# Routing ten tiles one iteration sooner, keeping three tiles dense, and running sorted tiles between the pieces of the last cross attention

## What is computed

```python
x = x + self_attention(layernorm(x))          # 16 heads, causal, rotation over the whole head vector
x = x + cross_attention(layernorm(x), ctx)    # 16 heads of 32, over 722 rows
h = layernorm(x)                              # then a mixture of 8 experts, 2 of them for each token
gates = softmax(h @ gate_w.T + gate_b)
top_gates, top_idx = top_k(gates, 2)
out = einsum('bsh,eoh->bseo', h, expert_w) + expert_b
x = x + (take(out, top_idx) * top_gates).sum()
```

## Time and profile before

| what | us |
|---|---|
| median of 3 runs | 1271.86 (1271.14 to 1278.15) |
| profiled execution | 1280.48 |
| its span, first to last instruction | 1278.7 |
| PE busy | 1194.4 (93%) |
| VectorE, GpSimd, ScalarE busy | 830.7, 729.6, 642.2 |
| DMA | 93.28 MB, mean 73 GB/s |

### The profile page before, as it was taken

One profiled execution on the slowest core, in us unless ns is written; L12 is line 12 of the kernel. 1 busy time (PEld: TensorE's weight loads), 2 busy tenths in 40 slices (PEclk: granted clock), 3 DMA queues, 4 the chain that ended last, 5 costly groups with the idle time before them and its releaser, 6 DMA issues.

```text
span 1278.7 us, 43327 instructions
## 1 busy us (share of the span) xinstructions
PE 1194.4 (93%) x19120; PEld 806.8 (63%) x19120; DVE 830.7 (65%) x1455; ACT 642.2 (50%) x946; POOL 729.6 (57%) x690
## 2 busy tenths in 40 slices
PE   4789899999999999999999999999999877699997
PEld 4456576767667676767676767676767555555543
DVE  4658476858585867676767777677777586423156
ACT  4335556556565656565656464646565535533300
POOL 1436656667676766667675857575757455500042
PEclk9799999999999999999999999999999988799999
DMA  8010611010202010101011110101010345455356
GB/s 302 2 42 2 240 44 50 3 59 3 66 4 65 17 44 9 53 17 52 19 50 32 38 48 12 43 17 52 17 58 11 116 159 190 146 159 170 131 163 212
DMA packets 47840, 93.28 MB, mean 73 GB/s; under 512 B 3775, under 2 KB 15351, under 8 KB 47655
## 3 DMA queue, kind: packets, MB, share of 16 engines
q1 hardware_dynamic: 44135, 79.03, 18.7%
q0 software_dynamic: 3520, 11.47, 2.9%
HBM read 60.13 MB, written 30.36 MB: 71 GB/s over the span
## 4 chain that ended last, share of the span: by engine, by line
PE 86%; DVE 4%; DMA 3%; POOL 3%; ACT 2%; issue 1%; another core or an unknown queue 1%; SPq 1%; ACTq 0%; DVEq 0%
PE psum L323 56%; PE psum L922 7%; PE psum L1025 6%; PE psum L1010 5%; PE psum L940 2%; PE psum L899 2%; PE psum L891 1%; DMA bank<-in_L_attn_Wv 1%; DMA out<-bank 1%; PE psum L967 1%; PE psum L855 1%; PE psum L907 1%; DVE xT L1176 1%; POOL bank L1444 1%
## 5 line engine op out<-in xcount | busy, mean ns | idle before, releaser
L1444 POOL TENSOR_TENSOR bank<-prob,bank 128x1200 f16<-128x1200 f32 x128 | 314.6, 2468 | 188.4 <-ACT bank L1120 188.3
L1268 DVE TENSOR_REDUCE c_most<-psum 100x4 f32<-100x1444 f32 x128 | 211.6, 1653 | 14.7 <-PE psum L1010 12.6
L323 PE MATMUL psum<-bank,cT 128*128 128x512 f16 (+1 forms) x864 | 198.7, 379 | 0.1
L323 PE MATMUL psum<-cT,bank 128*128 128x361 f16 x1152 | 196.1, 321 | 0.0
L1111 ACT ACTIVATE prob<-psum 128x1200 f32<-128x1200 f32 x128 | 150.0, 1172 | 76.6 <-PE psum L1025 62.4
L1176 DVE TENSOR_TENSOR cv<-psum,cv 128x512 f16<-128x512 f32 x125 | 86.0, 688 | 107.4 <-ACT cv L1102 57.2
L1120 ACT ACTIVATE bank<-prob 128x1200 f16<-128x1200 f32 x128 | 151.7, 1198 | 1.4
L323 PEld LDWEIGHTS psum<-cT,bank 128*128 128x128 f16 x1152 | 106.1, 99 | 65.5 <-DVE c_raw L1195 3.0
L323 PEld LDWEIGHTS psum<-bank,cT 128*128 128x128 f16 (+1 forms) x864 | 85.1, 101 | 88.2 <-issue 4.1
L1102 ACT ACTIVATE cv<-psum 128x512 f16<-128x512 f32 x96 | 57.4, 598 | 149.9 <-PE psum L323 148.3
L1229 DVE SCALAR_TENSOR_TENSOR bank<-psum,b_part,bank 128x361 f16<-128x361 f32 x128 | 74.4, 592 | 81.1 <-ACT bank L1088 81.1
(11 more groups left out here) (215 smaller groups left out, 1905.8 us busy)
## 6 DMA issues: line engine op xcount, KB each, us to landing
c_raw<-in_ctx SPq DMA_DIRECT2D x16, 960.0 KB
xs_scratch<-y_kept SPq DMA_DIRECT2D x1, 7424.0 KB, 22.8
c_raw<-xs_scratch SPq DMA_DIRECT2D x29, 256.0 KB, 2.7
ys_scratch<-bank SPq DMA_DIRECT2D x29, 256.0 KB, 2.0
...
y_kept<-x_scratch SPq DMA_DIRECT2D x10, 256.0 KB, 3.2
```

Source lines behind the costliest of these rows:

```text
L323: last = pe.matmul(out_ap, a(pa), b(pb), start=(i == 0 and j == 0), stop=(i == len(pairs) - 1 and j == 2))
L1268: dve.tensor_reduce(c_most[:, hf], score[0:L, :, 0:HC], AXIS.X, ALU.max).then_inc(max_done, 1)
L1444: pool.tensor_tensor(prob16[o % 2][:, (2 + part) * PT:(3 + part) * PT], prob[:, part], prob16[o % 2][:, part * PT:(part + 1) * PT], ALU.su ...
```

## The change

Tiles 0 to 9 are routed, tile 10 (tokens 1280 to 1399, 120 rows) becomes dense with 11 and 12. So there are 27 slot tiles and 24 dense pieces. Tile 9 gets FS, FN, FX and FL in iteration 13. RT, RP and FR stand in steps 0 to 6 of iteration 14, SC0 to SC6 in its steps 8 to 19, and SC7 to SC9 in steps 0 to 3 of iteration 15. FW ends in step 14 there. Then ST0 to ST5 and SM0 to SM3 stand in steps 15 to 19, between the last group's pieces. SM is now a chunk in the four shared banks, copied out half by ACT and half by DVE. FS10 is in step 2 of iteration 15, FS11 in step 16. On SP, tile 10's load comes behind the four expert loads of iteration 15, then a wait for all scatters, x's store, tile 11's load and the slot loads; the reloads 4 to 9 move to iteration 14. Tiles 10 to 12 have buffers of their own for their rows. Cut to its core:

```diff
-EARLY = 11
-EARLY_ROWS = B * L - 2 * L
-LATE = 2
+EARLY = 10
+EARLY_ROWS = EARLY * P
+LATE = 3
 TILES = EARLY + LATE
 SLOT_TILES = (2 * EARLY_ROWS + E * (P - 1)) // P
...
 def tile_rows(t):
 
     if t < EARLY:
-        return t * P, min(P, EARLY_ROWS - t * P)
-    return EARLY_ROWS + (t - EARLY) * L, L
+        return t * P, P
+    ends = (EARLY_ROWS, T - 2 * L, T - L, T)
+    return ends[t - EARLY], ends[t - EARLY + 1] - ends[t - EARLY]
 
...
+TURN_LATE = {15: ["FS9"], 16: ["FN9"], 18: ["FX9"], 19: ["FL9"]}
+GATE_EXTRA = {0: ["RT00", "RE0"], 1: ["RT01"], 3: ["RT02"], 5: ["RT03", "RP"], 6: ["FR"], 8: ["SC0"], 10: ["SC1"],
+              12: ["SC2"], 14: ["SC3"], 15: ["SC4"], 17: ["SC5"], 19: ["SC6"]}
 LAST_STEPS = [
-    ["low3a", "A0", "max_A0", "SC1", "FW00", "FW01"],
-    ["B0", "max_B0", "low3b", "FW02", "FW03"],
-    ["MX0", "SC2", "FW10"],
-    ["T0a", "exp0a", "PV3", "FW11", "PL"],
-    ["T0b", "exp0b", "high0a", "FW12", "FW13"],
-    ["A1", "max_A1", "low0a", "high0b", "FW20", "FW21"],
-    ["B1", "max_B1", "low0b", "scale_heads", "FW22", "FW23"],
-    ["MX1", "SC3", "FW30", "FW31"],
-    ["T1a", "exp1a", "SC4", "TT", "FW32"],
-    ["T1b", "exp1b", "high1a", "PV0", "FW33", "FW40"],
-    ["A2", "max_A2", "low1a", "high1b", "TP", "FW41"],
-    ["B2", "max_B2", "low1b", "FW42", "FW43"],
-    ["MX2", "SC5", "FW50", "FW51"],
-    ["T2a", "exp2a", "FS11", "SC6", "FW52", "FW53"],
-    ["T2b", "exp2b", "high2a", "PV1", "FN11", "FW60", "FW61"],
-    ["A3", "max_A3", "low2a", "high2b", "FW62", "FW63"],
-    ["B3", "max_B3", "low2b", "FX11", "FW70"],
-    ["MX3", "SC7", "FL11", "FW71"],
-    ["T3a", "exp3a", "SC8", "FW72", "FW73"],
-    ["T3b", "exp3b", "high3a", "PV2", "high3b", "SC9", "SC10"],
+    ["low3a", "A0", "max_A0", "SC7", "FW00", "FW01", "FW02"],
+    ["B0", "max_B0", "low3b", "FW03", "FW10", "FW11"],
+    ["MX0", "SC8", "FS10", "FW12"],
+    ["T0a", "exp0a", "PL", "SC9", "FW13"],
+    ["T0b", "exp0b", "PV3", "high0a", "FW20"],
+    ["A1", "max_A1", "low0a", "high0b", "FN10", "FW21", "FW22"],
+    ["B1", "max_B1", "low0b", "scale_heads", "FW23", "FW30"],
+    ["MX1", "FX10", "FW31", "FW32"],
+    ["T1a", "exp1a", "TT", "FL10", "FW33", "FW40"],
+    ["T1b", "exp1b", "high1a", "PV0", "FW41", "FW42"],
+    ["A2", "max_A2", "low1a", "high1b", "TP", "FW43", "FW50"],
+    ["B2", "max_B2", "low1b", "FW51", "FW52", "FW53"],
+    ["MX2", "FW60", "FW61", "FW62"],
+    ["T2a", "exp2a", "FW63", "FW70", "FW71"],
+    ["T2b", "exp2b", "high2a", "PV1", "FW72", "FW73"],
+    ["A3", "max_A3", "low2a", "high2b", "ST0", "ST1"],
+    ["B3", "max_B3", "low2b", "SM0", "ST2", "FS11"],
+    ["MX3", "SM1", "ST3", "FN11"],
+    ["T3a", "exp3a", "SM2", "ST4", "PV2"],
+    ["T3b", "exp3b", "SM3", "ST5", "high3a", "high3b"],
 ]
-END_EXTRA = {2: ["PV3", "scale_heads"], 5: ["TT"], 6: ["TP"], 9: ["FS12"], 10: ["FN12"], 11: ["FX12"], 12: ["FL12"],
-             13: ["RT10", "RE1"], 14: ["RT11"], 15: ["RT12"], 16: ["RT13"]}
-END_STEPS = [["low3a", "low3b", "ST0", "ST1"]] + [
-    ([f"ST{j + 2}"] if j + 2 < SLOT_TILES else []) + [f"SM{j}"] + END_EXTRA.get(j + 1, []) for j in range(SLOT_TILES)]
+DONE_SLOTS = 4
+END_EXTRA = {0: ["low3a", "low3b"], 2: ["PV3", "scale_heads"], 3: ["FX11"], 4: ["TT", "FL11"], 5: ["TP"], 8: ["FS12"], 9: ["FN12"],
+             10: ["FX12"], 11: ["FL12"], 12: ["RT10", "RE1"], 13: ["RT11"], 14: ["RT12"], 15: ["RT13"]}
+END_STEPS = [([f"ST{j + 2}"] if j + 2 < SLOT_TILES else []) + [f"SM{j}"] + END_EXTRA.get(j - DONE_SLOTS, [])
+             for j in range(DONE_SLOTS, SLOT_TILES)]
 
 
 def steps_of(n):
@@ -151,12 +150,13 @@
         return LAST_STEPS
     if n == B:
         return END_STEPS
-    every = [list(step) for step in (moved(STEPS, "TP", 7) if n == B - 2 else STEPS)]
+    every = [list(step) for step in STEPS]
     for t in range(EARLY - 1):
         if turn(t) == n:
             for h, name in ((2, "FS"), (3, "FN"), (5, "FX"), (7, "FL")):
                 every[h].append(f"{name}{t}")
-    extra = GATE_EXTRA if n == B - 2 else {2: ["FG0"], 7: ["BV0", "BV1"]} if n < 0 else {}
+    extra = (GATE_EXTRA if n == B - 2 else TURN_LATE if n == B - 3 else
+             {2: ["FG0"], 7: ["BV0", "BV1"]} if n < 0 else {})
     for h, names in extra.items():
         every[h] += names
...
 
-        def dense_count(i):
-
-            return sum(o[0] == "dense" for o in ORDER[:i + 1])
-
-        GATES_AT = SLOT_TILES + 1
+        GATES_AT = 1
         BIAS_FROM = len(ORDER) - TILES
         BIAS_ORDER = tuple(range(EARLY, TILES)) + tuple(range(EARLY))
 
...
             pe.wait_ge(chunk_out, ALL_CHUNKS)
-            for i in range(SLOT_TILES, len(ORDER)):
-                _, e, t = ORDER[i]
...
+            for i, (e, t) in enumerate(ORDER):
+                if i >= 4:
+                    pe.wait_ge(y_done, i - 3)
+                split3(pe, psum[0:y[t].shape[0], i % 4, 0:D],
+                       [(lambda p, k=k: xT3[t][:, p, k], lambda p, k=k: wT_all[:, e, k, p])
+                        for k in range(KD)]).then_inc(y_ready, 1)
                 if i == GATES_AT:
...
                    .then_inc(sum_done, 1)
 
             dve.wait_ge(chunk_out, ALL_CHUNKS)
-            for i in range(SLOT_TILES, len(ORDER)):
-                _, e, t = ORDER[i]
-                dve.wait_ge(y_ready, dense_count(i))
-                if dense_count(i) > LATE:
-                    dve.wait_ge(y_done, dense_count(i) - LATE)
-                dve.scalar_tensor_tensor(y[t], psum[0:L, i % 4, 0:D], g_scaled[0:L, t, e:e + 1], y[t],
+            for i, (e, t) in enumerate(ORDER):
+                r = y[t].shape[0]
...
             if t == EARLY:
                 pool.wait_ge(chunk_out, its[B - 1].all_before())
+            if t == TILES - 1:
+                pool.wait_ge(scattered[1], 32 * ((EARLY + 2) // 4))
...
@@ -752,6 +730,12 @@
                 end_loads(sp, it)
                 return
             turned = [t for t in range(EARLY - 1) if turn(t) == n]
+            if n == B - 2:
+                store_y(sp, EARLY - 1)
+                sp.wait_ge(y_stored, 16 * EARLY)
+                sp.wait_ge(chunk_out, its[B - 3].done(f"FL{EARLY - 1}"))
+                for t in range(4):
+                    load_again(sp, t)
             for t in turned:
                 load_y(sp, t)
             if n == B - 2:
@@ -763,22 +747,22 @@
                 sp.dma_start(x2_dram[n - 1], x_out[:]).then_inc(x2_stored, 16)
...
+            if n == B - 3:
+                load_y(sp, EARLY - 1)
             if n < B - 2:
                 sp.wait_ge(chunk_out, it.done("SO"))
                 load_ctx(sp, n + 2)
                 sp.wait_ge(chunk_out, it.done("OP"))
                 load_x(sp, n + 2)
             if n == B - 2:
-                load_y(sp, EARLY - 1)
-                store_y(sp, EARLY - 1)
-                sp.wait_ge(y_stored, 16 * EARLY)
-                sp.wait_ge(chunk_out, it.done(f"FL{EARLY - 1}"))
-                for t in range(4):
+                for t in range(4, 7):
                     load_again(sp, t)
                 sp.wait_ge(chunk_out, it.done("SO"))
                 load_expert(sp, E - 1)
                 sp.wait_ge(chunk_out, it.done("OP"))
                 load_expert(sp, 2)
+                for t in range(7, EARLY):
+                    load_again(sp, t)
 
         def last_loads(sp, it):
 
@@ -786,33 +770,36 @@
             sp.wait_ge(exp_done, 2 * GROUPS * (B - 1))
             for e in range(3, E - 1):
                 load_expert(sp, e)
-            for t in range(4, EARLY):
-                if t == 8:
-                    sp.wait_ge(chunk_out, it.done("TP"))
-                    sp.dma_start(x2_dram[B - 2], x_out[:]).then_inc(x2_stored, 16)
-                load_again(sp, t)
-                if t == 8:
-                    load_y(sp, EARLY)
-
-        def end_loads(sp, it):
-
+            load_y(sp, EARLY)
             all_scattered(sp)
-            sp.wait_ge(chunk_out, its[B - 1].done("FW73"))
+            sp.wait_ge(chunk_out, it.done("TP"))
+            sp.dma_start(x2_dram[B - 2], x_out[:]).then_inc(x2_stored, 16)
+            load_y(sp, EARLY + 1)
+            sp.wait_ge(chunk_out, it.done("FW73"))
             for j in range(4):
                 load_slots(sp, j)
-            for j in range(SLOT_TILES):
-                if j + 4 < SLOT_TILES:
-                    sp.wait_ge(chunk_out, it.done(f"ST{j}"))
-                    load_slots(sp, j + 4)
-                if j >= 2:
-                    store_slots(sp, j - 2)
-                if j == 4:
+            for j in range(DONE_SLOTS):
+                next_slots(sp, j)
+
+        def next_slots(sp, j):
+
+            if j + 4 < SLOT_TILES:
+                sp.wait_ge(chunk_out, where(f"ST{j}").done(f"ST{j}"))
+                load_slots(sp, j + 4)
+            if j >= 2:
+                store_slots(sp, j - 2)
+
+        def end_loads(sp, it):
+
+            for j in range(DONE_SLOTS, SLOT_TILES):
+                next_slots(sp, j)
+                if j == DONE_SLOTS + 4:
```

(37 more changed lines are left out.)

68 lines of the change are left out of this document (22 added, 46 removed).

## The result

The changed kernel takes 1293.34 us (median of 4 runs, 1292.86 to 1294.76) against 1272.97 of before in the same set: ratio 1.0155, interval 1.0123 to 1.0187, slower by about 20 us. Forecast was 1281, slower, with a range of 1261 to 1294. The sign and the main places of the loss were right; of its size less than half was seen, and the time lies only 0.7 us inside the range.

A forecast was written before the change was run, and what follows sets the result against it. PE was taken as full in sequence 13 and the end, losing time only in 14 and the last sequence. Terms +1.5 (13), +4.3 (14), +3.9 (last), -0.3 (products), -0.5 (tail) sum to +8.9 on 1271.9: 1281 us, range 1261 to 1294.

The forecast's parts named there:

- R3: Rival, chance 0.14: in sequence 14 every paired input meets POOL, MX1's split comes 15 us late, not 9; +10, 1291 us.
- The last sequence: Tile 10's load lands late behind four expert loads and holds DVE at FS10: 75.3 us, +3.9.
- Sequence 14: Two waits with their clock and tile 9 and 10 work leave, 62.3; 17.3 put in: 79.6 us, +4.3.
- (a): Sequence 14: RT00 and RT01 stand on DVE ahead of MX0's split, which T0a follows; +1.0 us.
- (b): Sequence 14, step 5: RT03 and RP, slowed beside POOL, stand ahead of max_B1; PE's MX1 waits +5.3 us.
- (c): Sequence 14: FR's placing stands ahead of MX1's split in step 7, beside low0b, delaying T1a; about +4.0 us.
- (e): Sequence 14: SC3 and SC4 together on POOL hold norm_mid and X2T; PE waits +2.4 us, its clock adds +1.6.
- (d): Sequence 14: PE's lowered clock after the two waits of (b) and (c); +3.0 us.
- Product work: The end: fewer sorted products and turnings against eight more dense pieces, split copy hidden; sum -0.3 us.
- R1: Rival, chance 0.20: finished pieces cover the routing in sequence 14; (b) to (e) fall from 16.3 to about 4; 1269 us.
- R2: Rival, chance 0.14: tile 10 lands before DVE asks and the routing is covered; another -8, 1261 us.
- R4: Rival, chance 0.52 together with the forecast: SM0 to SM3 wait for slots and run after the attention; 1288 us.

The follow-up runs named there:

- r0: The changed kernel run once more, nothing altered: 1296.43 us, ratio 1.0171.
- r5: Changed kernel with routing and scatters placed as in the kernel before, all sorted pieces in the end, tile 10 loaded ahead of the experts: 1286.78 us, ratio 1.0096.
- r6: As r5, but with the sooner routing of the change and seven scatters in sequence 14: 1291.66 us, ratio 1.0130.
- r1: Changed kernel with tile 10's load issued ahead of the four expert loads, not behind them: 1284.31 us, ratio 1.0084.
- r4: The unchanged kernel before, run for a second profile: 1275.16 us, ratio 1.0001; profiled execution 1271.79 us.
- r2: Changed kernel with tile 4's scatter one step later, behind norm_mid: 1292.82 us, ratio 1.0151.
- r3: Changed kernel with ST0 to ST5 and SM0 to SM3 moved back to the head of the end: 1301.64 us, ratio 1.0216.
- r8: As r1, with RT03 and RP moved from step 5 to 8, FR from 6 to 9, three scatters later: 1280.63 us, ratio 1.0047.
- r11: As r8, with the pieces between the last scores a step later, FR at step 10 for 9, and SC0 to SC4 later: 1283.17 us, ratio 1.0076.

## Why the prediction was right in its sign and short in its size

**In the range, in part by luck.** The signs set down for "right" came: FS10's idle time of 13.93 us, B1 at A0 + 28.3, comparisons of 2.53 and 2.13 us, idle time before MX1, T1a and X2T. But the time is 12.3 us over the forecast, in the band that the prediction gave to R3, and R3's mechanism did not happen. That the range took it in is the width of the range; r0's 1296.43 is beyond it.

**The sum by the runs.** Each step is a difference of ratios, of about 1273 us: the third dense tile +12 (before to r5), the sooner routing +4 (r5 to r6), the pieces between the scores -6 (r6 to r1), the late load +9 to +11 (r1 to the changed kernel). Together +20, which they must give, since each begins where the last ended; what they show is the shares. Each of these differences is known to 3 or 4 us.

**The base.** The prediction summed against a profiled execution that was over the median, and put the sum on the median. It knew the 8.6 us between them (7.5 by the median of the new set) and did not ask which stage held them. r4 shows it: 9.9 us in the last attention, 3.6 in sequence 14, less 3.7 given back at the end's start. The step that failed is in the last sequence: its forecast 75.3 us were set against 71.4, and those held the two stalls that r4 doesn't have. B1 to A2 was put at 10.0 and r4 has 10.9 already, where the first profile had 14.5; the last group's 23.4 were set against "21.9 before", which hold the stall of 7 us. Against r4 the changed kernel's last attention, up to its last turned score, is 18.6 us longer (77.3 for 58.75), and what follows is 1.4 shorter. What an ordinary execution doesn't lose, the change can't save. Of the 12.3 us by which the forecast was short 7.5 are this base, 1.1 the median of before in the new set, and 3.8 the terms below (12.7 us of span for 8.9). Since r4's execution is one of the quicker ones, the stall's share of the 7.5 is an estimate.

**The last sequence**, forecast 75.3, was 81.0. B1 came at A0 + 28.3 (forecast 27.3), A2 10.9 later (10.3), A3 15.2 later (14.3), and the last group took 26.6 (23.4). The cause, a load behind four experts on one queue, was right and r1 confirms it; it landed at A0 + 21.9 for 20.3. Of the load's 16.8 us SyncE's own issue took 4.0. The last group's term was mis-sized: the slots landed for ST0 4.23 us after PE was ready, where the sum had none, and SM0 ran at half clock, 4.69 us for 2.75, where the sum had 0.5 for the clock. That is 5.7 us for a miss of 3.2, so the rest of the group's timetable was some 2.5 too long.

The Trainium skill (DMA: Bandwidth & Descriptors, "Queues, rings and completion order") has a ring's descriptors consumed in order; 16.8 us behind four experts and 4.7 ahead of them agree.

**Sequence 14**, forecast 79.6, was 73.7, 78.0, 75.1, 75.9 and 74.9 in the profiles of the change, its second run, r1, r2 and r3. The forecast change was +4.3 on the first profile's 75.3; on the 71.7 of r4 it is +2 to +6. The 62.3 before anything is put in is borne out: r5, without the sooner routing, has 66.4, of which 3.2 are the wait at the split maximum and 1.7 its low clock, and 61.5 are left. Of the items put in, (a) measured 1.13 us for 1.0. (b) and (c), forecast 9.3, measured 5.95 (3.19 + 1.15 + 1.61). Their mechanism, POOL's instruction holding up a paired one of DVE, stands by the rows above and by r8 and r11. But (b) named MX1 as the victim; most of it fell on FR, which the prediction did not count among PE's work that needs the ranking, and r8 shows most of that wait (2.88 us) with 1.2 us of contention left where there had been 3.0. (e) was 2.12 us at X2T for 2.4, and in r2 a wait of 0.98 took part of its place. The clock, (d) and the rest of (e), was put at 4.6 and lost 3.4, half of 6.8 us. The prediction's 5.1 us for (b) and (c) without POOL's part doesn't follow from its own terms: 2.2, 1.2 and 2.3 taken from 9.3 leave 3.6.

The Trainium skill (SBUF — State Buffer, "Who interferes with whom") says that a VectorE instruction with two SBUF inputs contends with a GpSimd instruction that reads SBUF, by an exclusive lock on the ports that they share. The trace agrees, down to 128x8: 0.17 us alone, 2.15 beside POOL.

**Product work**, forecast -0.3, was +1.3 (156.1 for 154.5): 0.93 us is a wait at the first dense piece for a copy that the prediction held to be hidden. **Sequence 13**, +1.5, as forecast. **The tail**, -0.5, was +0.6.

**The rivals.** R1 and R2 are out: the routing was not covered ((b) to (e) cost 11.5 us with the clock, of 16.3 forecast and 4 under R1), the load was late. R3 is out by 73.7 us in sequence 14. R4 is out: SM0 to SM3 ran between the scores, and r3 and r6 put their worth at 6 to 8 us, near the 7.5 by which R4 was set over the forecast.

**What is open.** What the two exponentials of the first profile waited for; neither wait came again in r4. Why the low clock takes 6.8 us in one execution of the same sequence 14 and 17.1 in another. That the 0.4% from r5 to r6 is a loss and no accident is not settled. And no version here that keeps the third dense tile is as fast as before.
